# Message stage of a graph kernel: row numbers fetched ahead as I16, node columns compacted by ACT, and one-hots of the last pair built on ACT

## The reference

```python
row, col = (edges[0], edges[1])
x_tangent = logmap0(x)
x_local_tangent = logmap(x[row], x[col])
cat = jnp.concatenate([x_tangent[row], x_tangent[col], distances], axis=-1)
h = jax.nn.silu(cat @ att_w1 + att_b1)
att = jax.nn.sigmoid(h @ att_w2 + att_b2) * edge_mask
agg = jax.ops.segment_sum(x_local_tangent * att, row, num_segments=N) / NORM_FACTOR
```

## Time and profile before

| | us |
|---|---|
| median of three runs | 4436.49 (4432.94 to 4451.04) |
| the profiled execution | 4442.74 |
| its span | 4440.9 |

### The profile page before, as it was taken

One profiled execution on the slowest core, in us unless ns is written; L12 is line 12 of the kernel. 1 busy time (PEld: TensorE's weight loads), 2 busy tenths in 40 slices (PEclk: granted clock), 3 DMA queues, 4 the chain that ended last, 5 costly groups with the idle time before them and its releaser, 6 DMA issues. The chain is left out here.

```text
span 4440.9 us, 62303 instructions
## 1 busy us (share of the span) xinstructions
PE 2971.0 (67%) x12512; PEld 2322.0 (52%) x12513; DVE 3600.7 (81%) x9543; ACT 2112.1 (48%) x5629; POOL 2029.9 (46%) x2409
## 2 busy tenths in 40 slices
PE   1111211365778877787884688888888888889685
PEld 0100110354556655555653566676677777677463
DVE  6879999553899999999996478788888888888766
ACT  0003333001555555555555566566666666666465
POOL 1000000001777777777750076666666666666201
PEclk9999755687889999999997899999999999999897
DMA  0010000323777788887854376666666666666431
GB/s 7 0 38 0 0 0 0 99 81 114 243 239 240 239 241 241 241 240 240 241 176 134 111 221 183 182 177 182 177 184 181 179 179 180 182 180 188 120 73 47
DMA packets 294443, 664.28 MB, mean 150 GB/s; under 512 B 77026, under 2 KB 146336, under 8 KB 293870
## 3 DMA queue, kind: packets, MB, share of 16 engines
q0 software_dynamic: 141312, 463.96, 36.9%
q1 hardware_dynamic: 152813, 197.34, 15.9%
HBM read 616.23 MB, written 44.91 MB: 149 GB/s over the span
## 5 line engine op out<-in xcount | busy, mean ns | idle before, releaser
L2240 POOL DMA_INDIRECT big<-d_xr,ms_col x880 | 873.5, 993 | 724.8 <-DMA ms_col<-by_src_edge_cols 257.7
L1812 POOL DMA_INDIRECT big<-d_qv,at_col x880 | 940.5, 1069 | 561.4 <-DMA at_col<-by_dst_edge_cols 287.8
L2333 PE MATMUL ms_near_a<-big,ms_hotT 128*128 x1760 | 544.5, 391 | 77.6 <-issue 30.1
L2334 PE MATMUL ms_near_c<-big,ms_hotT 128*128 x1760 | 527.6, 381 | 0.0
L1838 PE MATMUL at_kx<-big 128*128 x1760 | 500.4, 411 | 32.5 <-ACT big L1912 22.9
L1858 PE MATMUL at_out<-at_pv,at_hot 128*128 128x264 f32 x1760 | 518.7, 421 | 3.8 <-DVE big L2024 2.3
L2353 PE MATMUL ms_out<-ms_more,ms_hot 128*128 128x257 f32 x1408 | 377.3, 391 | 106.6 <-DVE ms_hot L2472 106.3
L2333 PEld LDWEIGHTS ms_near_a<-big,ms_hotT 128*128 128x128 f32 x1760 | 321.9, 190 | 179.8 <-issue 139.2
L1838 PEld LDWEIGHTS at_kx<-big 128*128 128x128 f32 x1760 | 353.2, 206 | 113.7 <-issue 55.3
L1858 PEld LDWEIGHTS at_out<-at_pv,at_hot 128*128 128x128 f32 x1760 | 334.6, 203 | 69.0 <-issue 9.0
L2334 PEld LDWEIGHTS ms_near_c<-big,ms_hotT 128*128 128x128 f32 x1760 | 336.5, 191 | 49.5
(11 more groups left out here) (369 smaller groups left out, 5967.4 us busy)
## 6 DMA issues: line engine op xcount, KB each, us to landing
big<-by_dst_marks SPq DMA_DIRECT2D x110, 512.0 KB, 5.5
ms_hotT<-by_src_marks SPq DMA_DIRECT2D x110, 448.0 KB
big<-d_qv,at_col POOLq DMA_INDIRECT x880
big<-d_xr,ms_col POOLq DMA_INDIRECT x880, 4.5
d_qv<-big SPq DMA_DIRECT2D x5, 2240.0 KB, 9.1
ms_hotT<-by_src_marks SPq DMA_DIRECT2D x110, 60.0 KB
d_xr<-mid_hm SPq DMA_DIRECT2D x5, 1128.8 KB, 7.1
qkv_xt<-in_x_dram SPq DMA_DIRECT2D x5, 1120.0 KB, 14.3
```

What stands on the lines that cost most here:

```text
L1812: pool.indirect_dma_start(out=ring[t.slot][:, k, :], out_offset=None, in_=m.d_qv, in_offset=bass.IndirectOffsetOnAxis(ap=col[:, t.h, k, 0: ...
L2240: pool.indirect_dma_start(out=far_rows(t, p)[:, k, :], out_offset=None, in_=m.d_xr, in_offset=bass.IndirectOffsetOnAxis(ap=col[:, t.h, SPA ...
L2333: TE.matmul(near_a[:, (SPAN * p + k) % 4, 0:TW], rows, m.tab_a[:, bass.ds(at, TW)], start=True, stop=True)
L2334: last = TE.matmul(near_c[:, p % 2, k * DIM:(k + 1) * DIM], rows, m.tab_c[:, bass.ds(at, DIM)], start=True, stop=p % 2 == 0)
```

## The change

- Sort by source: the source numbers are also cast to I16 (`near_no`) on DVE, and this array is what goes to DRAM (`e.lk`), in place of the F32 one.
- SP fetches them into a buffer of their own (`near_no`, two slots), two turns ahead; only the weights row still goes into `hotT`, after that turn's hot columns are there. The column fetch now waits for `out_in` (PE's sums) in place of `weighted`.
- DVE builds the hot columns of turn t+2 at p = 3 from `near_no`, waiting for `near_in` of turn t; it no longer builds the hot rows of the last pair. PE waits for the weights row alone (`point_in`).
- ACT builds the hot rows of the last pair: |n - source| by Abs, 1 minus that by Relu, times the coefficient by Copy (`hot_rows_last`), between `squares(t, 2)` and `silu(t, 3)`.
- ACT copies each turn's two node columns of the differences into compact tiles (`take_columns`), so that `angles` on DVE has two 16-wide operations in place of six 8-wide ones.
- POOL's coefficients wait for `out_in` as well.

```diff
@@ -274,8 +275,12 @@
                 sp.wait_ge(ready, 3)
                 sp.dma_start(e.off.rearrange("o (j s) -> (o j) s", s=P), offT[:, :]).then_inc(lines_out, 16)
                 sp.wait_ge(cut, 1)
-                sp.dma_start(e.marks[0:1, P:P + N].rearrange("o (j s x) -> s (o j) x", s=P, x=span * P),
-                             part[:, 0].rearrange("s j i e -> s j (i e)")).then_inc(lk_out, 16)
+                if weighed:
+                    sp.dma_start(e.lk.rearrange("o (j s x) -> s (o j) x", s=P, x=span * P),
+                                 near_no.rearrange("s j i e -> s j (i e)")).then_inc(lk_out, 16)
+                else:
+                    sp.dma_start(e.marks[0:1, P:P + N].rearrange("o (j s x) -> s (o j) x", s=P, x=span * P),
+                                 part[:, 0].rearrange("s j i e -> s j (i e)")).then_inc(lk_out, 16)
...
@@ -419,6 +424,9 @@
                 ln.mark(V.tensor_tensor(join(part[:, 0]), join(part_i[:, 0]), lift_all, ALU.subtract))
                 ln.wait(1)
                 ln.mark(V.tensor_copy(part[:, 1], part_i[:, 1]))
+                if weighed:
+                    ln.wait(1)
+                    ln.mark(V.tensor_copy(near_no[:, :, :, :], part[:, 0]))
                 ln.wait()
                 dve.sem_inc(cut, 1)
                 cols_of = lambda n: scol[:, :, n].rearrange("e (x i) -> e x i", i=span)
@@ -2204,17 +2213,24 @@
                         return
                     old = t.plus(-BODY)
                     if old.exists():
-                        sp.wait_ge(weighted, old.n * G + G)
+                        sp.wait_ge(out_in, old.n * SG + SG)
                     sp.dma_start(col[:, t.h, :, :], edges.cols[:, bass.ds(t.n * G, G), :]).then_inc(col_in[t.h], 16)
+
+                def fetch_near(t):
+                    if not t.exists():
+                        return
+                    for rows in STRIPES:
+                        sp.dma_start(near_no[rows, t.h % 2, :],
+                                     edges.lk[:, bass.ds(t.n * (G * P), G * P)].to_broadcast([rows.stop - rows.start, G * P])).then_inc(no_in[t.h % 2], 16)
 
                 def fetch(t):
                     fetch_col(t.plus(4))
-                    if t.plus(-2).exists():
-                        sp.wait_ge(near_in, t.plus(-2).n * SG + SG)
-                    for rows in STRIPES:
-                        sp.dma_start(hotT[rows, t.h % 2, :], edges.lk[:, bass.ds(t.n * (G * P), G * P)].to_broadcast([rows.stop - rows.start, G * P])).then_inc(bc_in[t.h % 2], 16)
-                    sp.dma_start(hotT[ROWS:P, t.h % 2, :], edges.w[0:1, bass.ds(t.n * (G * P), G * P)]).then_inc(bc_in[t.h % 2], 16)
-
+                    sp.wait_ge(hotT_in, t.n + 1)
+                    fetch_near(t.plus(2))
+                    sp.dma_start(hotT[ROWS:P, t.h % 2, :], edges.w[0:1, bass.ds(t.n * (G * P), G * P)]).then_inc(point_in[t.h % 2], 16)
+
+                fetch_near(Turn(0, 0))
+                fetch_near(Turn(0, 1))
                 for h in range(4):
                     fetch_col(Turn(0, h))
                 each_turn(sp, fetch, 0)
@@ -2285,7 +2301,7 @@
                     settle()
                     assert ln.n == PER, ln.n
                     if w.plus(-BODY).exists():
-                        reach(weighted, (w.plus(-BODY).n + WG) * G)
+                        reach(out_in, (w.plus(-BODY).n + WG) * SG)
                     GP.tensor_tensor(cs[:, w.wslot, :], S, DEN, ALU.mult).then_inc(c_ready, 1)
 
                 def period(t):
@@ -2318,7 +2334,7 @@
                     at = starts.values(p % 2, 1)[0]
                     if p == 0:
                         pe.wait_ge(hotT_in, t.n + 1)
-                        pe.wait_ge(bc_in[t.h % 2], t.turns(2) * 48)
+                        pe.wait_ge(point_in[t.h % 2], t.turns(2) * 16)
                     before, q = pair_before(t, p, 2)
                     if before.exists():
                         pe.wait_ge(apart, before.n * SG + q + 1)
@@ -2344,7 +2360,10 @@
                         return
                     if p == 0:
                         pe.wait_ge(a_in, WG * t.window + WG)
-                    pe.wait_ge(weighted, t.n * G + SPAN * p + SPAN)
+                    if p == SG - 1:
+                        pe.wait_ge(weighted_last, (t.n + 1) * SPAN)
+                    else:
+                        pe.wait_ge(weighted, t.n * (G - SPAN) + SPAN * p + SPAN)
                     before, q = pair_before(t, p, 2)
                     if before.exists():
                         pe.wait_ge(summed, before.n * SG + q + 1)
@@ -2399,6 +2418,33 @@
                         at = (t.h % WG) * G + SPAN * p + k
                         AC.activation(junk[:, k, 1:DIM], dd[t.slot][:, SPAN * p + k, 1:DIM], ACT.Square,
                                       accum_out=SQ[:, t.wslot, at:at + 1]).then_inc(squared, 1)
+
+                def take_columns(t):
+
+                    if not t.exists():
+                        return
+                    if t.plus(-WG).exists():
+                        act.wait_ge(nn_in, t.plus(-WG).window + 1)
+                    k = slice((t.h % WG) * G, (t.h % WG) * G + G)
+                    AC.activation(Q[:, k], dd[t.slot][:, :, 0], ACT.Square).then_inc(taken, 1)
+                    AC.copy(BOTH[:, k], dd[t.slot][:, :, DIM]).then_inc(taken, 1)
+
+                def hot_rows_last(t):
+
+                    if not t.exists():
+                        return
+                    last = slice(G - SPAN, G)
+                    act.wait_ge(c_ready, t.window + 1)
+                    if t.plus(-1).exists():
+                        act.wait_ge(out_in, t.plus(-1).n * SG + SG)
+                    for k in range(G - SPAN, G):
+                        AC.activation(hot[:, k, :], m.ramp[:, :], ACT.Abs, scale=-1.0, bias=col[:, t.h, k, 1:2].bitcast(F32)).then_inc(spread, 1)
+                    act.wait_ge(spread, (t.n + 1) * SPAN)
+                    AC.activation(hot[:, last, :], hot[:, last, :], ACT.Relu, scale=-1.0, bias=one).then_inc(marked, 1)
+                    act.wait_ge(marked, t.n + 1)
+                    for k in range(G - SPAN, G):
+                        at = (t.h % WG) * G + k
+                        AC.activation(hot[:, k, :], hot[:, k, :], ACT.Copy, scale=cs[:, t.wslot, at:at + 1]).then_inc(weighted_last, 1)
 
                 def chain(w):
                     n = w.window
@@ -2424,10 +2470,12 @@
                     squares(t, 1)
                     silu(t, 2)
                     squares(t, 2)
+                    hot_rows_last(t.plus(-LATE))
                     silu(t, 3)
                     squares(t, 3)
-
-                each_turn(act, period, WG)
+                    take_columns(t)
+
+                each_turn(act, period, LATE)
 
             @block.vector
             def _(dve):
@@ -2438,7 +2486,7 @@
                 V.memset(m.acc_l1[:, 0:TW], 0.0).then_inc(made, 1)
                 dve.wait_ge(made, 3)
                 starts = Starts(dve, "ms_dve", off, (NB - 1) * TW, SG)
-                PER = 13
+                PER = 9
 
                 def differences(t, p):
                     if not t.exists():
@@ -2455,9 +2503,10 @@
 
                     if not t.exists():
                         return
-                    part = hotT[0:ROWS, t.h % 2, :]
-                    dve.wait_ge(bc_in[t.h % 2], t.turns(2) * 48)
-                    V.tensor_scalar(part, part, m.lane[0:ROWS, 0:1], None, ALU.is_equal).then_inc(hotT_in, 1)
+                    dve.wait_ge(no_in[t.h % 2], t.turns(2) * 32)
+                    if t.plus(-2).exists():
+                        dve.wait_ge(near_in, t.plus(-2).n * SG + SG)
+                    V.tensor_scalar(hotT[0:ROWS, t.h % 2, :], near_no[0:ROWS, t.h % 2, :], m.lane[0:ROWS, 0:1], None, ALU.is_equal).then_inc(hotT_in, 1)
 
                 def hot_rows(t, p):
 
@@ -2499,20 +2548,16 @@
                     n = w.window
                     ln = Links(dve, dv, n * PER)
                     sq, own = SQ[:, w.wslot, :], OWN
-                    groups = [(dd[t.slot], slice((t.h % WG) * G, (t.h % WG) * G + G)) for t in (w, w.plus(1))]
                     dve.wait_ge(squared, (w.n + WG) * G)
                     dve.wait_ge(copied, (w.n + WG) * SG)
+                    dve.wait_ge(taken, (w.n + WG) * 2)
                     if w.plus(-WG).exists():
                         dve.wait_ge(c_ready, n)
                         dve.wait_ge(a_in, WG * n)
-                    for rows, k in groups:
-                        ln.mark(V.tensor_tensor(Q[:, k], rows[:, :, 0], rows[:, :, 0], ALU.mult))
-                        ln.mark(V.tensor_tensor(own[:, k], rows[:, :, DIM], FARM[:, w.wslot, k], ALU.subtract))
-                    ln.wait()
+                    ln.mark(V.tensor_tensor(own, BOTH, FARM[:, w.wslot, :], ALU.subtract))
                     ln.mark(V.tensor_tensor(DD, sq, Q, ALU.subtract))
                     ln.wait()
-                    for rows, k in groups:
```

(27 more changed lines are left out.)

5 lines of the change are left out of this document (removed).

## The result

The changed kernel takes 4378.85 us, the kernel before, on the same chip, 4438.32. The 4378.85 is the median of four executions, of which one took 5065.23 us at a mean granted clock of 0.66, where the other three (4372.58 to 4381.48, median 4376.23) have 0.87 to 0.90; the ratio, 0.9857 [0.9828, 0.9886], is of the three. So it is faster by 59.5 us (62 by the three), where 143 were forecast (4295, with a range of 4210 to 4370): the sign was right, the size less than half, and the time lies outside the range. The profiled execution took 4372.58 us (span 4370.8), against 4442.74 before: -70.2. The final stage starts at 4120.46 us in place of 4187.58, so 67.1 us of it come from the message stage and what lies ahead of it.

The account below looks back on a forecast made before the run. DVE's wait for the weights row's DMA was taken to bound the kernel: 14.70 us a turn falling to 13.19, times 98 turns = 148, less 6 once = 142 us off; 4295 us, range 4210 to 4370.

Parts of the forecast that it names:

- What bound before: Message stage: DVE waits nearly every turn for the weights row's DMA, a loop DVE, SP, DMA; 14.70 us a turn.
- put at 1.83: ACT, ahead of silu of pair 3: two Abs, a Relu and two Copies for the last pair's hot rows take 1.83 us.
- rival 3: ACT: Abs and Relu force table loads between silus, 2.6 us a window, about 4422 us; chance 0.04.
- The weights row is covered: SP to PE: the row's path takes 5.9 us against 6.1 of cover, so it costs 0.
- rivals 2 and 4: Weights row late for PE: up to 1.35 a window, about 4361 us (chance 0.20); or much later, about 4579 (0.05).
- by some 2 us: Sign to look for: PE's near L2333 waits for ACT once a window, by some 2 us.
- rival 1: The silu loop does not bite, DVE or PE decide: 12.4 us a turn, about 4217 us; chance 0.14.
- the sum 26.37: Loop over each window (two turns) through DVE, ACT's silu of pair 3 and PE: 26.37 us, 13.19 a turn.
- 11.61 + 0.70 + 2.47: PE's nears and sums 11.61, hand-over and difference on DVE 0.70, v of pair 0 to ACT's table load 2.47.
- 8.97 + 1.83: ACT: table load to silu of pair 3 without its radii wait, 8.97, plus the last pair's hot rows, 1.83.
- 0.36 for shorter angles: DVE: four fewer operations in the angles save 0.36 us a window, also taken off the way to the table load.
- the 6 of once each: One-time costs: cast in the sort +0.7, first weights row 4, tail through ACT +1; sum +6 us.

Follow-up runs that it names:

- e5: Kernel before with the prefetch of integer row numbers alone, nothing moved to ACT, no compact columns: 4262.34 us.
- e12: Kernel before with ACT's order alone changed, silus of pairs 2 and 3 ahead of squares of pairs 1 and 2 in chain turns: 4444.62 us.
- e4: Kernel after with SP issuing the large stripe of prefetched row numbers behind the weights row: 4372.34 us.
- e8: Kernel after with hot rows behind silu of pair 3 and, in chain turns, silus of pairs 2 and 3 ahead of squares of pairs 1 and 2: 4224.96 us.
- e11: e8 without the compact columns, DVE reading the strided columns itself: 4215.9 us.
- e1: Kernel after with DVE building all hot rows again, prefetch and compact columns kept: 4284.8 us.
- e2: Kernel after with ACT building the last pair's hot rows just after silu of pair 3: 4268.42 us.
- e10: e5 with silus of pairs 2 and 3 ahead of squares of pairs 1 and 2 in chain turns, nothing moved to ACT: 4227.46 us.
- e3: Kernel after with three unused 128-wide activations on ACT ahead of the last pair's hot rows in every turn: 4508.25 us.
- e9: Kernel after with eight unused 128-column matmuls on PE ahead of the near product of pair 1 in every odd turn: 4390.36 us.
- e7: e3 with eight unused 128-column matmuls on PE ahead of the near that waits: 4442.36 us.

## Why the prediction was right and wrong

*What bound before: right.* e5 takes the loop DVE, SP, DMA away and moves nothing to ACT, and gains 182 us; e12 changes ACT and gains nothing.

*The parts: mostly right.* DVE's waits for the DMA are gone. Hot columns from I16 take 0.747, where 0 was taken for the change and 0.5 kept as the bound. The Trainium skill, "VectorE: DVE Perf Modes", section "What auto-detection actually checks", sets no condition on the type for the two-port mode of a one-source operation in SBUF; the trace agrees (0.747 with I16 in, 0.753 with F32 in). `hot_rows_last` was put at 1.83 and takes 1.85 (3438.28 to 3440.13). No table load came with it (rival 3), as the Trainium skill, "ScalarE: Activation LUTs", section "Table sets: the hidden batching unit", says. The weights row is covered, as taken (e4; rivals 2 and 4 are out). The silu of pair 3 does hold PE up once a window, "by some 2 us": 2.63. So the kind of loop was forecast rightly, and rival 1, that it doesn't bite, is wrong for this kernel. Its 12.4 a turn is nearly met by e8 (12.53) and e11 (12.43), where ACT's order takes the loop away.

*The step that failed* is the sum 26.37 and its use. Against the trace:

| term | forecast | trace |
|---|---|---|
| near of pair 1 to the table load (11.61 + 0.70 + 2.47) | 14.78 | 15.72 |
| table load to silu of pair 3 (8.97 + 1.83) | 10.80 | 10.63 |
| silu, to PE | 0.79 | 0.79 |
| window | 26.37 | 27.14 |
| a turn | 13.19 | 13.57 |

The first term is wrong in its path, not in a row. I entered ACT's chain by DVE: v of pair 0, angles, table load. But in ACT's order the silu of pair 1 stands before the chain, and it waits for PE's near of pair 1. That near ends at 3428.83, the load starts at 3429.58. So 3413.86 to 3428.83 is 14.97, and 0.75 for the silu: 15.72, 0.94 over the forecast. In the rows of before the silu of pair 1 had its input early, as DVE was the late one, and so I left the link out. The second term ran 0.17 under.

The same path has a second fault. The 2.47 is the 2.83 of before less 0.36 for shorter angles, but that stretch does not run through the angles. In the kernel before the load of 3440.38 follows ACT's silu of pair 1, and DVE starts the last operation of the angles only after it:

```profile
3439.78 0.59 ACT L2384 ACTIVATE big<-ms_near_c 128x512 f32<-128x512 f32 x1
```

```profile
3441.17 0.18 DVE L2530 TENSOR_SCALAR big<-big 128x16 f32<-128x16 f32 x1
```

So shorter angles could not bring the load forward. In the kernel after v of pair 0 starts at 3426.02 on DVE, and from there to the load it is 3.56. Of the 0.94 the wait for PE makes 0.73 (3.56 less 2.83), the 0.36 had no place, and the way to v gives 0.15 back (12.16 for 12.31).

The last fault is in the units. 14.70 was a mean over ten-turn iterations and the 13.19 a sum of links within one. The iteration's end costs 2.39, 0.24 a turn, and the window with a fallen clock 1.83, 0.18 a turn. 13.57 + 0.24 + 0.18 = 13.99, against the 13.95 measured. With that the gain is 0.75 x 98 = 73, less the 6 of once each: 67, the shift of the final stage, 67.1. That this meets is in part luck. PE's first near product starts 0.9 us earlier than before (2559.0), its first and last lie 1530.0 us apart in place of 1593.9, and from the last one to the final stage it is 31.5 in place of 33.8: 0.9, 63.9 and 2.3 are the 67.1. So the turns brought 64 and not 73, and of the 6 us only the cast in the sort is seen (0.69), while the start and the tail that the forecast made dearer came out cheaper. Of the 0.76 us a turn that were missing (13.95 less 13.19), the entry made half (0.38) and the iteration's end with the clock the other half (0.42 by the one iteration). That the 2.39 is wholly the loop's end is read from one iteration; the others between 2767 and 3750 us take 139.2 to 140.6, but for one of 143.7.

*One sum for the whole change* hid a better reading: the same numbers said that hot rows ahead of silu of pair 3 cost up to 1.83 a window, about 90 us. e1 and e2 measured 94 and 110. The forecast carried that term inside the 13.19 and never set it against the 0.51 a turn that it freed on DVE, which was not the bound.

*Columns.* I took 0.36 a window as gained. By e1 against e5 they cost 22 us; e8 against e11 gives 9, which is not clear of noise.

## What to carry to other kernels

When a wait is taken out of a loop, follow the next loop link by link through every engine's own order, also through links whose input was early before: they are late next. Here work that was moved to an idle engine cost nothing as load and much as place: the same five activations were worth +94 us ahead of a silu that PE waits for (the kernel after against e1), and -12 to -16 us behind it (e11 against e10, e2 against e1). And sum like with like: a mean over iterations can't be compared with a sum of single instances, which leaves the iteration's end out.

## What the hardware showed beside that

PE's granted clock fell from 1.00 to 0.50 (from the 2.4 to the 1.2 GHz level) behind pauses of 3.50 us, in nearly every window of e3, and stayed low over some 6 us of full work (3433.26 to 3439.55). Pauses of 2.63 and 2.78 us mostly left it at 1.00 (kernel after, behind 2907.05), and pulled it down for some 4 us in one to three windows of an iteration, mostly the first behind its end (3018.00). Meanwhile two matmuls took 1.06 us in place of 0.59. A delay of 0.88 us on ACT thereby cost 3.7 us of 27.1. Where PE is idle for another reason than the clock, filling the pause bought nothing (e9); where the pause itself was long, it bought 66 us (e7 against e3).

The length of the one pause does not decide it alone. In the kernel after the matmuls behind a pause of 2.98 us (2981.89) took 0.59 and those behind one of 2.88 us (3544.71) 1.06. In e2 a shorter one was enough:

```profile
3085.50 1.53 PE L2372 MATMUL ms_out<-ms_more,ms_hot 128*128 128x257 f32 x4 [2.31 <-DVE ms_hot L2521]
3086.82 1.06 PE L2349 MATMUL ms_near_a<-big,ms_hotT 128*128 x2
```

And in e3 the pause of 3.50 us at 3525.66 left them at 0.59. What else decides was not tried.
